# A Mamba layer and an fp8 feed-forward layer on one core: waits of the first stage reordered, twelve states of C loaded two batches earlier

## The chip, the core and the metric
The kernel runs on one core of a Trainium2 chip. Its time is the device time of one execution in microseconds (us). TensorE (PE) multiplies, VectorE (DVE), ScalarE (ACT) and GpSimd (POOL) work element by element, SyncE (SP) issues the DMA transfers. The engines run side by side and wait for each other through semaphores.

## What is computed
x has the shape (4, 512, 512): batches, positions, features. The result is x plus a Mamba layer of the normalized x plus a gated feed-forward layer of the normalized x. Cut to what matters:

```python
xn = layernorm(x)
# Mamba: DI 1024, N 16 states, R 128
proj = einsum('blh,eh->bel', xn, Win); hs, gate = proj[:, :DI], proj[:, DI:]
hs = silu(conv4(hs) + bconv)                      # causal, 4 taps, per channel
ssm = einsum('bdl,pd->blp', hs, Wx)               # dt_in (128), B (16), C (16)
dt = softplus(einsum('blr,dr->bld', dt_in, Wdt) + bdt)
h_t = exp(A * dt_t) * h_(t-1) + dt_t * B_t * hs_t # for each channel and state
y = (sum_n h * C + hs * D) * silu(gate)
out = x + einsum('bdl,hd->blh', y, Wout)
# feed-forward in fp8, HIDDEN 2048
out += qdot(gelu(qdot(xn, w_g0)) * qdot(xn, w_g1), w_lin)
```

## The kernel before, in words
The program has two stages. The first (`stage_a`) makes, for each of the 4 batches `b`, the transposed normalized x (`xnT`), the projection `hs` of 8 units `k` of 128 channels, the convolution, silu, the small projections (`dt_ps` for dt, `bc_ps` for B and C), and `dt` and `dt*hs` (`dt_du`). It stores them in DRAM. The second (`stage_b`) walks over batches, units and 16 states: a scan on VectorE for each state (line 1125), with exp on ScalarE (`da`) and `dt*hs*B` on GpSimd (`dbu`).

Products in the first stage are made of a high and a low part of each operand (`products`): ScalarE makes the high parts (`hs_hi`, `xnT_hi`), the low parts (`hs_lo`, `xnT_lo`) are differences, made by GpSimd but for the start. In a batch TensorE makes units 2 to 7 of the projection, three units ahead of the products `ssm_inputs(k)` of hs; then dtin is copied (ScalarE, line 597), and the softplus stretch follows: for each unit TensorE makes z (`project_dt`), VectorE `capped`, ScalarE Exp and Ln, VectorE `dt_du` (line 495), GpSimd its product with hs (`du`, line 378), SP the store. `dt_du` has four slots; `dt_du(k)` waits for the store of `dt_du(k-4)`. Beside it TensorE begins the next batch's projection: tile h of unit 0 after z of unit h+2, then units 1 and 2.

Every transfer is issued by SP, in the order in which its program is written, on one queue. In a batch before the change: the store of xnT (1 MB), for units 0, 3 and 6 a `chunk` (store of the converted fp8 weights `w8`, 256 KB, and load of the next `wf`, 1 MB, which VectorE converts behind its convolutions of units 1, 4 and 7, line 473), for each unit the store of hs (256 KB), xn8, bc, the eight stores of dt_du (512 KB each), the load of four states of B (`b_head`, 1 MB). In the last batch six loads of C of batch 0 (`c_head`, two states and 512 KB each) and two of `unit` (768 KB) are interleaved. `c_head` holds the rows of x of batches 1 to 3 (`x_rest`) until they are normalized, four states of it for each batch.

At the end of the first stage GpSimd makes the first six `dbu` of the second (`head_start`, three instructions, line 858) ahead of its last eight du. `deviation` is the square root of the variance `vare` of the next batch; its function lies in another table of ScalarE than silu.

## Time and profile before

| | |
|---|---|
| median of 3 runs | 1058.67 us (1058.31 to 1058.89) |
| profiled execution | 1060.56 us, its span 1058.8 us |
| VectorE busy | 994.5 us (94%) |
| GpSimd busy | 913.0 us (86%) |
| TensorE busy | 910.5 us (86%) |
| ScalarE busy | 832.8 us (79%) |
| granted TensorE clock, mean | 0.956 |
| first scan of the second stage | 206.07 us |

The span runs from the first to the last instruction of the profiled execution. A busy share is a mean over both stages; the granted clock is the share of full speed that TensorE had.

### The profile page before, as it was taken

The page shows a single profiled execution, that of the slowest core. Times are in us where ns is not written, and L with a number is a line of the kernel's source. Part 1 is how long each engine was busy: PE and PEld are TensorE (multiplying, and loading weights), DVE is VectorE, ACT ScalarE, POOL GpSimd, SP SyncE. Part 2 cuts the span into 40 slices and gives each one's busy share as a digit, 9 for nine tenths or more (in the row PEclk, how much of TensorE's full clock was granted, in tenths as well). Part 3 has the DMA queues.
Part 4 walks back from the last instruction along what each step waited for, and adds up shares of the span by engine and source line. Part 5 has one row for each costly group of instructions (what it writes and reads, how often), then busy time and mean ns, then how long its engine had stood idle before and what let it go on. Part 6 is the DMA issues. An engine that isn't in the chain of part 4 may idle for free.

```text
span 1058.8 us, 14443 instructions
## 1 busy us (share of the span) xinstructions
PE 910.5 (86%) x4328; PEld 561.2 (53%) x4328; DVE 994.5 (94%) x1190; ACT 832.8 (79%) x1164; POOL 913.0 (86%) x512
## 2 busy tenths in 40 slices
PE   5888989577789987998799879887998798879998
PEld 4656757244445554554455556554555455445554
DVE  6887878799999999999999999999999999999996
ACT  5888987688888666898896668988866689888662
POOL 4566674899999899899999998999899989998993
PEclk9999999889889998999999979998999899999999
DMA  8678879991112129232121292221213922212101
GB/s 305 219 264 281 302 264 345 377 334 55 61 41 90 40 75 332 107 103 80 60 90 41 97 346 88 86 80 60 90 41 115 350 78 75 80 59 81 41 1 40
DMA packets 53208, 150.26 MB, mean 142 GB/s; under 512 B 5776, under 2 KB 14096, under 8 KB 50064
## 3 DMA queue, kind: packets, MB, share of 16 engines
q1 hardware_dynamic: 53136, 149.41, 40.6%
q8 instruction: 32, 0.52, 0.2%
q14 instruction: 40, 0.33, 0.1%
HBM read 111.37 MB, written 38.01 MB: 141 GB/s over the span
## 4 chain that ended last, share of the span: by engine, by line
DVE 32%; issue 25%; POOL 17%; ACT 11%; PE 7%; DMA 6%; SPq 1%; DVEq 1%; POOLq 0%; ACTq 0%
POOL dbu L858 11%; DVE da L1125 11%; DVE prod L1100 8%; DVE hp L1125 6%; POOL hp L1088 4%; DMA wf<-in_wffn 3%; ACT da L1019 2%; DVE conv L445 2%; PE yT L1251 2%; ACT L1008 1%; ACT L1007 1%; DVE gate_bf L1138 1%; DVE y L1108 1%; PE mm L1200 1%; DMA b_all<-bc_d 1%
## 5 line engine op out<-in xcount | busy, mean ns | idle before, releaser
L1019 ACT ACTIVATE da<-unit,neg_a 128x512 f32<-128x512 f32 x512 | 338.6, 684 | 156.9 <-DVE prod L1100 154.0
L858 POOL TENSOR_TENSOR dbu<-unit,b_head 128x1024 f32<-128x1024 f32 x192 | 450.0, 2367 | 0.0
L1125 DVE TENSOR_TENSOR_SCAN da<-da,dbu 128x512 f32<-128x512 f32 x352 | 417.9, 1218 | 1.3
L1251 PE MATMUL yT<-ident,prod 128*128 128x128 f32 x1408 | 227.7, 291 | 93.0 <-DVE prod L1100 92.2
L1251 PEld LDWEIGHTS yT<-ident,prod 128*128 128x128 f32 x1408 | 168.2, 147 | 227.7 <-DVE prod L1100 188.2
L1088 POOL TENSOR_TENSOR hp<-hp,c_head 128x512 f32<-128x512 f32 x128 | 162.7, 1271 | 50.7 <-DVE gate_bf L1141 46.1
L1125 DVE TENSOR_TENSOR_SCAN hp<-da,dbu 128x512 f32<-128x512 f32 x160 | 193.5, 1210 | 3.3 <-ACT da L1019 3.3
L1100 DVE TENSOR_TENSOR prod<-da,c_head 128x512 f32<-128x512 f32 x256 | 171.7, 671 | 0.0
L1200 PE MATMUL mm<-xn_b,w_sb 128*128 128x512 fp8e4 x512 | 143.8, 414 | 15.9 <-ACT acc L1039 12.9
L858 POOL TENSOR_TENSOR dbu<-unit,b_all 128x1024 f32<-128x1024 f32 x64 | 151.0, 2359 | 0.0
L1212 PE MATMUL mm<-xnT_b,wgate 128*128 128x512 f32 x256 | 128.8, 601 | 0.0
L1160 PE MATMUL mm<-y,wout_sb 128*128 128x512 f32 x242 | 114.6, 593 | 0.8 <-DVE y L1108 0.8
L1251 PE MATMUL yT<-ident,hp 128*128 128x128 f32 x640 | 98.9, 278 | 0.0
L1200 PEld LDWEIGHTS mm<-xn_b,w_sb 128*128 128x128 fp8e4 x512 | 51.5, 105 | 66.0 <-issue 34.7
L362 POOL TENSOR_TENSOR hs_lo<-hs,hs_hi 128x512 fp32r<-128x512 f32 x32 | 41.8, 1307 | 44.8 <-ACT hs_hi L568 44.8
L445 DVE SCALAR_TENSOR_TENSOR conv<-proj,cols_sb,conv 128x511 f32<-128x511 f32 (+2 forms) x96 | 71.0, 746 | 8.7 <-ACT conv L550 6.3
L1251 PEld LDWEIGHTS yT<-ident,hp 128*128 128x128 f32 x640 | 77.6, 145 | 0.0
L1160 PEld LDWEIGHTS mm<-y,wout_sb 128*128 128x128 f32 x242 | 43.4, 190 | 43.0 <-issue 41.9
L1100 DVE TENSOR_TENSOR prod<-da,c_all 128x512 f32<-128x512 f32 x96 | 65.0, 678 | 0.0
L1221 PE MATMUL mm<-act,w_sb 128*128 128x512 fp8e4 x256 | 61.8, 379 | 0.0
L625 PE MATMUL proj<-xnT_lo,win_hi 128*128 128x512 f32 x128 | 57.0, 446 | 0.2 <-DVE conv L445 0.2
L378 POOL TENSOR_TENSOR dt_du<-dt_du,hs 128x512 f32<-128x512 f32 x32 | 40.9, 1283 | 13.0 <-DVE dt_du L495 12.4
(123 smaller groups left out, 1285.8 us busy)
## 6 DMA issues: line engine op xcount, KB each, us to landing
unit<-unit_d SPq DMA_DIRECT2D x32, 768.0 KB, 4.2
unit_d<-dt_du SPq DMA_DIRECT2D x32, 512.0 KB, 2.9
wf<-in_wffn SPq DMA_DIRECT2D x12, 1024.0 KB, 7.1
c_head<-bc_d SPq DMA_DIRECT2D x24, 512.0 KB, 4.1
b_head<-bc_d SPq DMA_DIRECT2D x18, 512.0 KB, 4.9
unit_d<-hs SPq DMA_DIRECT2D x32, 256.0 KB, 6.6
w_sb<-w_d SPq DMA_DIRECT2D x64, 128.0 KB, 3.8
wgate<-in_win_gate SPq DMA_DIRECT2D x32, 256.0 KB, 2.7
```

The costliest lines, as they stand in the source:

```text
L445: ins = nc.vector.scalar_tensor_tensor(out=conv[:, k % 2, back:L], in0=proj[k % 3][:, 0:L - back], scalar=cols_sb[:, k, C_TAP + TAPS - 1 - ...
L625: nc.tensor.matmul(bank, hi, low, start=start, stop=False)
L858: return nc.gpsimd.tensor_tensor(dbu[:, n % DBUS:n % DBUS + NS, :], twice, b_all[n // NS], ALU.mult)
L1019: nc.scalar.activation(da[n % SLOTS][:, :], unit[:, k % 2, 0, :], ACT.Exp, scale=neg_a[:, k, n:n + 1]).then_inc(da_ready, 1)
L1088: nc.gpsimd.tensor_tensor(tile, tile, c_all[m // NS][:, m % NS, :], ALU.mult).then_inc(hp_ready, 1)
L1100: nc.vector.tensor_tensor(prod[:, slot, :], da[n % SLOTS][:, :], c_all[n // NS][:, n % NS, :], ALU.mult).then_inc(prod_ready, 1)
L1125: nc.vector.tensor_tensor_scan(state, da[n % SLOTS][:, :], dbu[:, n % DBUS, :], 0.0, ALU.mult, ALU.add).then_inc(scanned, 1)
L1160: return nc.tensor.matmul(bank[:, :], wout_sb[:, c, h * P:(h + 1) * P], y2[:, c, :], start=(c == first), stop=(c == last))
L1200: ins = nc.tensor.matmul(bank[:, :], wffn[:, k % 2, j, f, s, :].bitcast(FP8), xn8[:, f, :].bitcast(FP8), start=(f == 0), stop=(f == HT - 1))
L1212: ins = nc.tensor.matmul(bank[:, :], wgate[:, k % 2, c * P:(c + 1) * P], xnT[:, c, :], start=(c == 0), stop=(c == 3))
L1221: ins = nc.tensor.matmul(bank[:, :], wlin[:, i, h * P:(h + 1) * P].bitcast(FP8), act8[:, i, :].bitcast(FP8), start=(i == 0), stop=(i == HI ...
L1251: ins = nc.tensor.matmul(yT[k % 2][:, t * P:(t + 1) * P], product[:, t * P:(t + 1) * P], ident[:, :], start=False, stop=last, is_transpose ...
```

## The change
Four edits concern waits. SP's chunk of unit 0 comes before the store of xnT (in the last batch the xnT store comes at unit 3, and the second `unit` load at unit 4). ScalarE makes the deviation at the start of a batch, behind the tap of unit 1, with one table load less. The copies of the last xnT tile move behind two units of the softplus stretch, on ScalarE, and its low part behind two du, on GpSimd. In batches 2 and 3 the low part of hs of unit 7 is made by VectorE. Besides, the six loads of C leave the last batch: four are issued in batch 1 and two in batch 2, behind the store of hs of unit 6. SP's loop over batches is written out.

```diff
--- before.py
+++ after.py
@@ -295,25 +295,27 @@
                         wait(dt_du_stored[i], 16 * (B - 1) * (KU // DTS) + 16)
                     wait(win_split, KU)
                     wait(xn_used, B)
-                wait(xnT_ready, b * HT + HT + 2)
-                sp.dma_start(row(xnT_d, b), xnT[:, :, :].rearrange("p k l -> p (k l)")).then_inc(xnT_stored, 16)
                 for k in range(KU):
                     if k % 3 == 0:
                         chunk(k // 3)
+                    if k == (3 if last else 0):
+                        wait(xnT_ready, b * HT + HT + 2)
+                        sp.dma_start(row(xnT_d, b), xnT[:, :, :].rearrange("p k l -> p (k l)")).then_inc(xnT_stored, 16)
                     if k == KU - 1:
                         wait(xn8_ready, b + 1)
                         sp.dma_start(row(xn8_d, b), xn8[:, :, :].rearrange("p k l -> p (k l)")).then_inc(xn8_stored, 16)
                     wait(hs_ready, b * KU + k + 1)
                     sp.dma_start(row(unit_d, b * KU + k)[:, 2 * L:3 * L], hs[:, k, :]).then_inc(hs_stored[k % 2], 16)
-                    if last and k >= 2:
-
-                        g = k - 2
-                        sp.dma_start(c_head[:, g * NS:(g + 1) * NS, :].rearrange("p n l -> p (n l)"),
-                                     bc_d[0:1, N + g * NS:N + (g + 1) * NS, :].rearrange("o n l -> o (n l)").broadcast_to([P, NS * L])
-                                     ).then_inc(c_loaded[g], 16)
-                    elif last:
-
-                        u = k
+                    if k == 6 and 1 <= b < B - 1:
+
+                        wait(xn_ready, 2 * b + 4)
+                        for g in range(2 * G_PER_B) if b == 1 else range(2 * G_PER_B, G_AHEAD):
+                            sp.dma_start(c_head[:, g * NS:(g + 1) * NS, :].rearrange("p n l -> p (n l)"),
+                                         bc_d[0:1, N + g * NS:N + (g + 1) * NS, :].rearrange("o n l -> o (n l)").broadcast_to([P, NS * L])
+                                         ).then_inc(c_loaded[g], 16)
+                    if last and k in (0, 4):
+
+                        u = k // 4
                         sp.dma_start(unit[:, u, :, :].rearrange("p w l -> p (w l)"), row(unit_d, u)).then_inc(unit_loaded[u], 16)
                 wait(bc_copied, b + 1)
                 sp.dma_start(row(bc_d, b), bc[:, :]).then_inc(bc_stored, 16)
@@ -328,7 +330,8 @@
                                  bc_d[0:1, bass.ds(first, states), :].rearrange("o n l -> o (n l)").broadcast_to([P, states * L])
                                  ).then_inc(b_head_loaded, 16)
 
-            run_batches(sp, body)
+            for b in range(B):
+                body(b, b == B - 1)
             for stored in (xnT_stored, xn8_stored):
                 wait(stored, 16 * B + 16)
             wait(w8_stored, 16 * CHUNKS + 16)
@@ -357,6 +360,8 @@
 
             def body(b, last):
                 for k in range(KU):
+                    if k == KU - 1 and b >= B - 2:
+                        continue
                     pool.wait_ge(hs_hi_ready, b * KU + k + 1)
                     pool.wait_ge(ssm_summed, b * KU + k + 1)
                     nc.gpsimd.tensor_tensor(hs_lo[:, k % 2, :], hs[:, k, :], hs_hi[:, k % 2, :], ALU.subtract).then_inc(hs_lo_ready, 1)
@@ -367,15 +372,20 @@
                             ins = nc.gpsimd.tensor_scalar(xn[:, t, :], x_rest[:, b * LT + t, :], moments[:, t, 0:1], rstd[:, t:t + 1],
                                                           ALU.subtract, ALU.mult)
                         ins.then_inc(xn_ready, 1)
+                def low_tile(h):
+                    pool.wait_ge(xnT_ready, (b + 1) * HT + h + 1 + 2)
+                    nc.gpsimd.tensor_tensor(xnT_lo[:, h, :], xnT[:, h, :], xnT_hi[:, h, :], ALU.subtract).then_inc(lo_ready, 1)
+
                 if not last:
-                    for h in range(HT):
-                        pool.wait_ge(xnT_ready, (b + 1) * HT + h + 1 + 2)
-                        nc.gpsimd.tensor_tensor(xnT_lo[:, h, :], xnT[:, h, :], xnT_hi[:, h, :], ALU.subtract).then_inc(lo_ready, 1)
+                    for h in range(HT - 1):
+                        low_tile(h)
                 if last:
                     head_start(pool)
                 for k in range(KU):
                     pool.wait_ge(dt_ready, b * KU + k + 1 + KU)
                     nc.gpsimd.tensor_tensor(dt_du[:, k % DTS, 1, :], dt_du[:, k % DTS, 0, :], hs[:, k, :], ALU.mult).then_inc(du_ready, 1)
+                    if k == 1 and not last:
+                        low_tile(HT - 1)
 
             for b in range(B):
                 body(b, b == B - 1)
@@ -462,6 +472,11 @@
                 for k in range(KU):
                     if k > 0:
                         convolve(b, k)
+                    if k == KU - 1 and b >= B - 2:
+                        dve.wait_ge(hs_hi_ready, b * KU + k + 1)
+                        dve.wait_ge(ssm_summed, b * KU + k + 1)
+                        dve.wait_ge(hs_lo_ready, b * KU + k)
+                        nc.vector.tensor_tensor(hs_lo[:, k % 2, :], hs[:, k, :], hs_hi[:, k % 2, :], ALU.subtract).then_inc(hs_lo_ready, 1)
                     if k == 3 and not last:
                         scales(b + 1)
                     if k in (1, 4, 7):
@@ -567,9 +582,13 @@
                     act.wait_ge(ssm_summed, b * KU + k + 1)
                     nc.scalar.activation(hs_hi[:, k % 2, :], hs[:, k, :], ACT.Copy).then_inc(hs_hi_ready, 1)
 
+                newest_tap(b, 1)
+                if not last:
+                    deviation(b + 1)
                 nc.scalar.preload_act_table_set("silu_and_others")
                 for k in range(1, KU):
-                    newest_tap(b, k)
+                    if k > 1:
+                        newest_tap(b, k)
                     if k == 5 and not last:
                         act.wait_ge(scales_ready, b + 2)
                         act.wait_ge(xn_used, b + 1)
@@ -579,9 +598,6 @@
                         ins.then_inc(xn_ready, 1)
                     silu(k - 1)
                     high_part(k - 1)
-                    if k == 2 and not last:
-                        deviation(b + 1)
-                        nc.scalar.preload_act_table_set("silu_and_others")
                     if k == 4:
                         fp8_copy(b)
 
@@ -597,9 +613,9 @@
                 nc.scalar.activation(dtin[:, :], dt_ps[:, :], ACT.Copy).then_inc(dtin_copied, 1)
                 nc.scalar.activation(bc_low[:, :], bc_ps[2 * N:4 * N, :], ACT.Copy).then_inc(bc_low_copied, 1)
                 nc.scalar.preload_act_table_set("natural_log_exp_and_others")
-                if not last:
-                    copy_tiles(b + 1, HT - 1, HT)
                 for k in range(KU):
+                    if k == 2 and not last:
+                        copy_tiles(b + 1, HT - 1, HT)
                     act.wait_ge(z_ready, b * KU + k + 1)
                     nc.scalar.activation(soft[:, k % 3, :], soft[:, k % 3, :], ACT.Exp).then_inc(exp_done, 1)
                     act.wait_ge(exp_done, b * KU + k + 1)
```

ScalarE, start of batch 0, before: the table load, the tap of unit 1 (`conv<-proj`), silu and high part of units 0 and 1, then the deviation between its two table loads.
```order
L570 ACT_TABLE_LOAD
L550 ACTIVATE conv<-proj,cols_sb 128x512
L563 ACTIVATE hs<-conv 128x512
L568 ACTIVATE hs_hi<-hs 128x512
L550 ACTIVATE conv<-proj,cols_sb 128x512
L563 ACTIVATE hs<-conv 128x512
L568 ACTIVATE hs_hi<-hs 128x512
L525 ACT_TABLE_LOAD
L525 ACTIVATE sd<-vare 128x4
L584 ACT_TABLE_LOAD
```
After:
```order
L565 ACTIVATE conv<-proj,cols_sb 128x512
L540 ACT_TABLE_LOAD
L540 ACTIVATE sd<-vare 128x4
L588 ACT_TABLE_LOAD
L578 ACTIVATE hs<-conv 128x512
L583 ACTIVATE hs_hi<-hs 128x512
L565 ACTIVATE conv<-proj,cols_sb 128x512
L578 ACTIVATE hs<-conv 128x512
L583 ACTIVATE hs_hi<-hs 128x512
L565 ACTIVATE conv<-proj,cols_sb 128x512
```
The deviation with both loads stands ahead of the first silu (`hs<-conv`), and one load is gone.

SP, end of batch 1: the transfers from the load of the last chunk on, before (the loop's body, the same for batches 0 to 2):
```order
L262 DMA wf<-in_wffn 128x2048
L254 REGISTER_ALU
L307 ISA
L307 DMA unit_d<-hs 128x512
L254 REGISTER_ALU
L305 DMA xn_d<-xn 128x2048
L254 REGISTER_ALU
L307 ISA
L307 DMA unit_d<-hs 128x512
L319 ISA
L319 DMA bc_d<-bc 32x512
```
After, batch 1:
```order
L262 DMA wf<-in_wffn 128x2048
L308 DMA unit_d<-hs 128x512
L313 DMA c_head<-bc_d 128x1024 x4
L306 DMA xn_d<-xn 128x2048
L308 DMA unit_d<-hs 128x512
L321 DMA bc_d<-bc 32x512
L324 DMA unit_d<-dt_du 128x1024 x8
L329 DMA b_head<-bc_d 128x2048
```
Four loads of C stand ahead of the stores of xn8, of hs of unit 7, of bc and of all dt_du.

VectorE, end of the last batch: the last convolution (three instructions), the conversion of the last weights, the sum of B and C, before:
```order
L445 SCALAR_TENSOR_TENSOR conv<-proj,cols_sb,conv 128x511
L445 SCALAR_TENSOR_TENSOR conv<-proj,cols_sb,conv 128x510
L445 SCALAR_TENSOR_TENSOR conv<-proj,cols_sb,conv 128x509
L473 TENSOR_SCALAR w<-wf 128x2048
L489 TENSOR_TENSOR bc<-bc_ps,bc_low 32x512
```
After:
```order
L455 SCALAR_TENSOR_TENSOR conv<-proj,cols_sb,conv 128x511
L455 SCALAR_TENSOR_TENSOR conv<-proj,cols_sb,conv 128x510
L455 SCALAR_TENSOR_TENSOR conv<-proj,cols_sb,conv 128x509
L479 TENSOR_TENSOR hs_lo<-hs,hs_hi 128x512
L488 TENSOR_SCALAR w<-wf 128x2048
L504 TENSOR_TENSOR bc<-bc_ps,bc_low 32x512
```
hs_lo stands between the convolution and the conversion.

## Rows read from the trace of the kernel before

**Rows 1.** Windows: us, busy PE, PEld, DVE, ACT, POOL, PEclk, DMA share, GB/s
```profile
206.00:1059.00 853.00, 739.44 (x3656) 442.34 (x3656) 835.90 (x941) 670.47 (x922) 784.98 (x415) 0.95 0.31 105
```

**Rows 2.** Timeline of VectorE: start us, us, line, operation [idle before, releaser]
```profile
19.34 1.91 DVE L438 TENSOR_TENSOR wx_lo<-wf,wx_hi 128x1024 fp32r<-128x1024 f32 x1 [1.60 <-ACT wbc L544]
...
27.23 0.17 DVE L405 TENSOR_SCALAR vare<-moments 128x4 f32<-128x4 f32 x1
...
55.04 0.97 DVE L405 TENSOR_SCALAR vare<-moments 128x4 f32<-128x4 f32 x1
...
178.06 1.23 DVE L473 TENSOR_SCALAR w<-wf 128x2048 fp8e4<-128x2048 f32 x1 [4.35 <-DMA wf<-in_wffn]
...
201.27 0.75 DVE L495 SCALAR_TENSOR_TENSOR dt_du<-dt_ps,cols_sb,soft 128x512 f32<-128x512 f32 x1 [1.68 <-DMA unit_d<-dt_du]
...
206.07 1.22 DVE L1125 TENSOR_TENSOR_SCAN da<-da,dbu 128x512 f32<-128x512 f32 x1
```

**Rows 3.** Timeline of TensorE: products of hs that begin a batch, transposes
```profile
30.27 0.47 PE L625 MATMUL dt_ps<-hs_lo,wx_hi 128*128 128x512 f32 x1 [2.80 <-POOL hs_lo L362]
...
76.62 0.47 PE L625 MATMUL dt_ps<-hs_lo,wx_hi 128*128 128x512 f32 x1 [0.47 <-POOL hs_lo L362]
...
93.40 1.03 PE L620 MATMUL tp<-ident,unit 128*128 128x128 f32 x8
...
121.64 0.40 PE L625 MATMUL dt_ps<-hs_lo,wx_hi 128*128 128x512 f32 x1
...
166.35 0.39 PE L625 MATMUL dt_ps<-hs_lo,wx_hi 128*128 128x512 f32 x1
```

**Rows 4.** Timeline of ScalarE: table load, silu, dtin copies, last tile, Ln, deviation
```profile
25.41 1.28 ACT L570 ACT_TABLE_LOAD   x1
...
27.39 0.62 ACT L563 ACTIVATE hs<-conv 128x512 f32<-128x512 f32 x1
...
55.03 0.60 ACT L597 ACTIVATE dtin<-dt_ps 128x512 f32<-128x512 f32 x1 [0.93 <-PE bc_ps L666]
...
101.14 0.60 ACT L597 ACTIVATE dtin<-dt_ps 128x512 f32<-128x512 f32 x1 [1.11 <-PE bc_ps L666]
...
103.67 0.60 ACT L514 ACTIVATE xnT_hi<-tp 128x512 fp32r<-128x512 f32 x1
...
115.52 0.63 ACT L606 ACTIVATE soft<-soft 128x512 f32<-128x512 f32 x1
...
123.50 0.21 ACT L525 ACTIVATE sd<-vare 128x4 f32<-128x4 f32 x1
...
145.81 0.60 ACT L597 ACTIVATE dtin<-dt_ps 128x512 f32<-128x512 f32 x1 [0.89 <-PE bc_ps L666]
...
190.15 0.60 ACT L597 ACTIVATE dtin<-dt_ps 128x512 f32<-128x512 f32 x1 [2.25 <-PE bc_ps L666]
```

**Rows 5.** DMA of the window 168 to 192 us
```profile
DMA packets 2457, 9.36 MB, mean 390 GB/s; under 512 B 270, under 2 KB 270, under 8 KB 1974
```

**Rows 6.** Timeline of SP: last w8 store of batch 1
```profile
98.77 0.33 SPq L287 DMA_DIRECT2D w_d<-w  x1
```

**Rows 7.** DMA of the window 103 to 104 us; issue, KB, us to landing
```profile
DMA packets 31, 0.25 MB, mean 254 GB/s; under 512 B 0, under 2 KB 0, under 8 KB 0
...
bc_d<-bc SPq DMA_DIRECT2D x1, 64.0 KB, 4.6
```

**Rows 8.** DMA issued between 99.0 and 99.6 us
```profile
wf<-in_wffn SPq DMA_DIRECT2D x1, 1024.0 KB, 6.5
```

**Rows 9.** Timeline of GpSimd: low part of the weights, of xnT, head start
```profile
17.61 2.56 POOL L356 TENSOR_TENSOR win_lo<-win_rest,win_hi 128x512 fp32r<-128x512 f32 x2 [3.15 <-ACT win_hi L532]
...
53.46 3.75 POOL L373 TENSOR_TENSOR xnT_lo<-xnT,xnT_hi 128x512 fp32r<-128x512 f32 x3
...
188.61 7.96 POOL L858 TENSOR_TENSOR dbu<-unit,b_head 128x1024 f32<-128x1024 f32 x3
```

**Rows 10.** Windows of TensorE, 32 to 34 us: busy (products), clock, DMA share, GB/s
```profile
32.00:34.00 2.00, 2.00 (x6) 0.50 0.94 242
```

## The prediction
> **What bounds the kernel now.** I read the windows first, to split the span. From 206 us on, VectorE is busy 835.90 of 853 us, against 739 on TensorE, 785 on GpSimd and 670 on ScalarE [rows 1]: the second stage runs at VectorE's own pace. It begins with the first scan at 206.07 [rows 2]. No edit touches its orders, so the change is worth what it moves that first scan by. The profiled execution took 1060.56 us beside its span of 1058.8; it stands 1.9 us above the median of the runs, 1058.67. I make the sum within the span and put the difference on the median. A measurement here tells 0.2%, some 2.1 us, from no change.
>
> Within the first stage I read the timeline of each engine. Every batch has two parts. From the first product of a unit's hs on TensorE (S) to the end of the last projection TensorE never waits: from 76.62 to the transposes at 93.40, where 1.14 of that is the fifth group of products (their pitch in the rows around), so S plus 15.65 us [rows 3]. Behind that the last unit goes through tap, convolution, silu, high part, low part and products to the copy of dtin (D). Behind D comes the softplus stretch, in which ScalarE, VectorE, TensorE and the stores of dt_du form one ring of four slots, until the next S. The rows give S = 30.27, 76.62, 121.64, 166.35 and D = 55.03, 101.14, 145.81, 190.15 [rows 3, 4]. So D to S takes 21.6, 20.5, 20.5, and S to D 24.8, 24.5, 24.2, 23.8. The last D to the first scan is 15.9.
>
> **Part by part, in order of time.**
>
> *Batch 0, the deviation first.* Before, the table load at 25.41 ends at 26.7 and the first silu starts at 27.39 [rows 4]. Now the tap comes at 25.41 (0.67), a load of 1.28, then sd. It waits for vare, written at 27.23 + 0.17 [rows 2]; sd 0.2 [rows 4], a second load 1.28: first silu at 28.95, +1.55. TensorE was waiting for just this unit (2.80 idle before 30.27) and runs full behind it, so S0 and D0 move by +1.55.
>
> *Softplus stretch.* Before, the last tile's copies stand at 103.67, two of 0.6 with a pitch of 0.97, ahead of the first Exp [rows 4]. Moved behind two units they let dt_du(0) come 0.9 sooner. TensorE, then VectorE and ScalarE pass on some 0.7: the last Ln ends at D + 14.3 instead of D + 15.0 (115.52 + 0.63 against 101.14). GpSimd's fourth low tile (1.25) fits behind du(1), since TensorE asks for it at D + 9.0. Behind the last Ln ScalarE now has tap 0.67, two loads and sd 2.8, silu 0.66, high part 0.7, then GpSimd 1.3: S at D + 20.6. In the last batch there is one load only, and TensorE is later: D + 19.9. The two loads that vanish in the middle of a batch, around the sd at 123.50 [rows 4], lay beside a full TensorE and are worth nothing; were TensorE not full there, they would be worth up to 2.6. Batch 0 had 21.6, so it gains 1.0; S1 comes at +0.55.
>
> *Weight chunk.* VectorE waited 4.35 for a chunk at 178.06 [rows 2], and less in the two batches before. The xnT store (1 MB) leaves its way. At 390 GB/s, the rate of the full queue from 168 to 192 [rows 5], that is 2.6 us sooner; in batch 1 the chunk now lands before VectorE asks. The last batch then follows TensorE again. The tail from the last projection to D is 7.3 (batch 0 has 7.4, with nothing in its way) against 8.9 in batch 1: -1.55. So D1 = -1.0.
>
> *C in batches 1 and 2: the disputed cost.* The rows of batch 1: the w8 store issues at 98.77, the bc store issues just behind 103 and lands 4.6 us later, at 107.9 [rows 6, 7]. Four loads of C (512 KB, 1.3 us each at the same rate) are put ahead of xn8, hs(7) and bc: 5.2 us. (SP's new wait for xn passes at once: xn of the next batch is made two units earlier.) The queue is then empty at D + 11.35; the first dt_du store goes behind it and lands 1.3 later, D + 12.65. Its slot is wanted by dt_du(4) at D + 10.0. That ring turns 2.6 late: dt_du(4) ends at D + 13.3, the last Ln at D + 16.6, z of unit 7, which waits for dt_du(4), starts at D + 13.3 on TensorE, and S at D + 23.2. Against 20.5 that is +2.65. S2 = +1.65.
> In batch 2 only two C loads come, 2.6 us. But the hs_lo that VectorE takes over stands ahead of its last w8, so the w8 store moves from D - 2.85, where batch 1 will have it, to D - 0.15, and the queue is again full until D + 11.3. dt_du(4) waits for D + 12.6, TensorE's z likewise, and three projections (8.2) end at D + 22.4: +1.85. In return hs_lo itself takes 0.7 instead of 1.3 to 1.5 there, and the wait for the chunk is gone: the tail is 6.75 against 8.6, -1.85. D2 = -0.2, S3 = +1.65.
>
> *Last batch.* The tail: GpSimd, freed of the last hs_lo, starts its head start (three dbu, 7.96 in all, the first of them held up) at once instead of at 188.61 [rows 9]. It begins 3.35 behind the last projection; VectorE wants its hs_lo at 4.5. Does GpSimd hold it up? wx_lo, 1024 elements on VectorE with both inputs in SBUF, started at 19.34 and took 1.91, with GpSimd's win_lo in SBUF until 17.61 + 2.56 = 20.17: what is left is 1.08. And vare took 0.97 at 55.04 beside a row of GpSimd's xnT_lo, 0.17 at 27.23 [rows 2, 9]. So I take it that hs_lo waits for the end of the first dbu (2.34), runs 0.7 and ends 6.4 behind the projection. D3 is then 7.85 behind it against 8.15: -0.3. If it didn't wait, 6.6: -1.55.
> The Trainium skill has a rule for it (SBUF — State Buffer, Who interferes with whom): a VectorE instruction with two SBUF inputs and a GpSimd one that reads SBUF fully block each other, and the first to issue wins. By that rule the sum is the one with the wait; the rows agree.
> From D3 on: before, dt_du(4) waited 1.68 for the first store, at 201.27; that store's du stood behind the head start, which ends at 196.57 [rows 2, 9], with C loads in the queue ahead of it. Now the head start ends by D + 4.5, no C is in the queue, the store lands by D + 9.3, and dt_du(4) is wanted at D + 9.4. The first scan comes at D + 14.25 against 15.92: -1.67.
>
> **Sum**: +1.55 - 1.0 - 1.55 + 2.65 - 1.85 + 1.85 + (S3 to D3) -0.3 - 1.67 = -0.3 us (rounded). SP's unrolled loop saves a few tenths of issue time per batch, hidden behind the same full queue; its cover gone it is worth 0.3. Forecast 1058.67 - 0.35 = **1058.3 us**: what the four changes give, about 4, C's new place takes back.
>
> **The rivals.**
> *C hides (faster).* The chunk ahead of C's new place took 6.5 us from issue for 1 MB [rows 8], where the full queue's rate makes 2.6: the queue has holes there, and C may fill them. In the window from 103 on it moved 254 GB/s, not 390 [rows 5, 7]. All bytes at 390 GB/s from the w8 store on: 4.06 MB, 10.4 us, the queue is empty at D + 9.2 and dt_du(4) waits 0.5 instead of 2.6; in batch 2, 0.65. Then D1 to S2 is 20.9 and D2 to S3 20.5, the sum -4.4: 1054.3. Against it: in the batches before each small store behind a chunk landed with it, in order, so C would begin only behind it. The Trainium skill says that descriptors of a ring start in order but are pipelined (DMA: Bandwidth & Descriptors, Queues, rings and completion order). By that this rival is possible; no row settles it.
> *TensorE's clock falls (slower).* After 2.80 us idle at 27.5 the granted clock fell from 30.9 to 34.3; at 32 it is 0.50, 1.2 GHz instead of 2.4, six products in 2 us instead of nine [rows 3, 10]. That costs half of 3.4 us, 1.7. With dt_du(4) 2.6 late TensorE idles 2.65 between z(6) and z(7), in batches 1 and 2. If it falls in both, +3.4: 1061.7; in one, 1060.0. [...]
> *hs_lo isn't held up*: -1.25, 1057.0, within "no change". The deviation's +1.55 in batch 0 could be less only if vare came sooner, which nothing does.
>
> **Chances.** Forecast with its own range 1056.6 to 1059.8: 0.50. C hides, in part or all: 0.30. Clock falls at least once: 0.18. The rest 0.02. Most of the forecast's range lies within 0.2%, 0.06 of it is faster; partial cases of the clock in one batch fall on the edge. So faster 0.36, same 0.46, slower 0.18, and the range from 1054.4 to 1060.8 leaves out about one in ten on each side.
>
> **What would show it.** The changed profile: first silu near 28.9; no wait of VectorE for a chunk in batch 1; dt_du in batches 1 and 2 waiting some 2 us for its store (if not, C hides); hs_lo on VectorE in the last batch about 1.9 long (0.7 would refute the blocking); the granted clock between D and S of batches 1 and 2; no wait for a store behind the last D; the first scan at 205.7. Wrong would make it above all a queue that doesn't keep order, or a second stage that isn't the same length (852.7 from the first scan on).

## The result: 0.7% slower

The changed kernel took 1066.01 us (median of 4, 1065.75 to 1069.42) against 1058.78 us for the kernel before on the same chip: ratio 1.0073, interval 1.0055 to 1.0090. A second measurement (run after_again, below) gave 1.0075, 1.0062 to 1.0088. The forecast was 1058.3 us, with a range up to 1060.8: the loss is real, 7 to 8 us, and lies outside it.

The profiled execution of the changed kernel is a long one of its kind, 1069.42 us with a span of 1067.3. Single executions of one kernel differ here: the kernel before took 1057.5 to 1061.7 us in 25 runs. So the profiles say where the time goes, and the medians say how much of it is real.

First the page after, its row of the clock over 40 equal slices of the span (a digit is the granted clock in tenths, 9 stands for 0.9 or more), then the window of the second stage (as in [rows 1]) and VectorE's timeline around the last batch's end (start us, us, line, operation, idle before and its releaser; as in [rows 2]):

```profile
PEclk9899998978899998999989988999999899989999
```

```profile
214.70:1067.00 852.30, 741.97 (x3646) 443.79 (x3656) 835.80 (x941) 670.55 (x922) 785.11 (x415) 0.95 0.31 105
```

```profile
114.55 0.75 DVE L510 SCALAR_TENSOR_TENSOR dt_du<-dt_ps,cols_sb,soft 128x512 f32<-128x512 f32 x1 [2.34 <-DMA unit_d<-dt_du]
...
162.81 0.75 DVE L510 SCALAR_TENSOR_TENSOR dt_du<-dt_ps,cols_sb,soft 128x512 f32<-128x512 f32 x1 [2.82 <-DMA unit_d<-dt_du]
...
196.24 1.69 DVE L479 TENSOR_TENSOR hs_lo<-hs,hs_hi 128x512 fp32r<-128x512 f32 x1 [1.36 <-ACT hs_hi L583]
197.86 3.39 DVE L488 TENSOR_SCALAR w<-wf 128x2048 fp8e4<-128x2048 f32 x1
201.17 0.67 DVE L504 TENSOR_TENSOR bc<-bc_ps,bc_low 32x512 f32<-32x512 f32 x1
...
214.78 1.22 DVE L1141 TENSOR_TENSOR_SCAN da<-da,dbu 128x512 f32<-128x512 f32 x1
```

The first scan stands at 214.78 instead of 206.07 [rows 2], and VectorE is as busy behind it as before, 835.80 us against 835.90 [rows 1]. So all of it is lost in the first stage. As in the prediction, D is the start of a batch's copy of dtin and S the first product of the next unit's hs, each with the number of its batch. dt_du(4) waits for its store in batches 1 and 2, 2.34 and 2.82 us, and starts at D + 12.5 and D + 13.0: this step stands as forecast (D + 12.65, D + 12.6). The next view shows what I had only as a rival. These are TensorE's windows (us, busy time, products, granted clock, DMA share, GB/s):

```profile
28.00:30.00 2.00, 0.00 (x0) 0.95 0.00 0
30.00:32.00 2.00, 0.00 (x0) 0.50 0.07 27
32.00:34.00 2.00, 1.66 (x4) 0.50 1.09 231
...
114.00:116.00 2.00, 0.65 (x1) 0.78 1.04 424
116.00:118.00 2.00, 2.00 (x4) 0.50 0.88 354
118.00:120.00 2.00, 2.00 (x9) 0.87 0.97 393
...
162.00:164.00 2.00, 0.39 (x1) 0.73 1.02 418
164.00:166.00 2.00, 2.00 (x4) 0.50 0.91 369
...
168.00:170.00 2.00, 2.00 (x7) 0.57 0.52 209
```

Behind each of the two waits the clock stands at 0.50, 1.2 GHz, with six products or fewer in 2 us; before, it stood there only in batch 0 [rows 10] and from 205 us on. TensorE's own rows at those places, and the first product of batch 0:

```profile
32.34 0.76 PE L641 MATMUL dt_ps<-hs_lo,wx_hi 128*128 128x512 f32 x1 [5.55 <-POOL hs_lo L367]
...
115.35 2.08 PE L689 MATMUL dt_ps<-dtin,wdt_sb 128*128 128x512 f32 x2 [2.39 <-DVE dt_du L510]
...
163.61 2.08 PE L689 MATMUL dt_ps<-dtin,wdt_sb 128*128 128x512 f32 x2 [2.87 <-DVE dt_du L510]
```

In batch 0 TensorE idles 5.55 us where it idled 2.80 [rows 3]. ScalarE's timeline of that place, and the four copies of dtin (D; before in [rows 4]):

```profile
23.78 0.63 ACT L547 ACTIVATE win_hi<-win_rest 128x512 fp32r<-128x512 f32 x1 [0.84 <-DMA win_rest<-in_win_hs]
...
25.10 1.28 ACT L540 ACT_TABLE_LOAD   x1
27.64 0.20 ACT L540 ACTIVATE sd<-vare 128x4 f32<-128x4 f32 x1 [1.25 <-DVE vare L415]
27.86 1.28 ACT L588 ACT_TABLE_LOAD   x1
29.15 0.63 ACT L578 ACTIVATE hs<-conv 128x512 f32<-128x512 f32 x1
...
57.51 0.60 ACT L613 ACTIVATE dtin<-dt_ps 128x512 f32<-128x512 f32 x1 [0.94 <-PE bc_ps L682]
...
102.08 0.60 ACT L613 ACTIVATE dtin<-dt_ps 128x512 f32<-128x512 f32 x1 [0.92 <-PE bc_ps L682]
...
149.84 0.60 ACT L613 ACTIVATE dtin<-dt_ps 128x512 f32<-128x512 f32 x1 [0.29 <-PE bc_ps L682]
...
199.46 0.60 ACT L613 ACTIVATE dtin<-dt_ps 128x512 f32<-128x512 f32 x1 [2.65 <-PE bc_ps L682]
```

The first silu, at 29.15, is within 0.2 us of the forecast. But the load of weights ahead of it landed a microsecond sooner in this execution (win_hi at 23.78, before at 24.76), so silu stands 5.37 behind that cast (`win_hi`) where it stood 2.63: measured from there, the edit costs ScalarE 2.7, not 1.55.

With S = 32.34, 78.92, 127.31 and 175.88 the profiled stage goes so, term by term (us, measured difference of the two profiles):

| stretch | forecast | measured |
|---|---|---|
| to S0 | +1.55 | +2.07 |
| S0 to D0 | 0 | +0.41 |
| D0 to S1 | -1.0 | -0.18 |
| S1 to D1 | -1.55 | -1.36 |
| D1 to S2 | +2.65 | +4.73 |
| S2 to D2 | -1.85 | -1.64 |
| D2 to S3 | +1.85 | +5.50 |
| S3 to D3 | -0.3 | -0.22 |
| D3 to the first scan | -1.67 | -0.60 |
| sum | -0.3 | +8.71 |

The three tails (S to D) are right within 0.2 in this execution. The stretches that begin at D carry the miss: 7.6 of the 9.0 us beyond the forecast.

The first tail did not come out so each time. In the profiled execution of after_again, the same kernel once more, D0 to S1 took 22.47 us and S1 to D1 24.74, 1.1 and 1.6 more than here. VectorE's conversion of a weight chunk, GpSimd's first hs_lo of batch 1, TensorE's product behind it, and TensorE's window:

```profile
77.60 1.22 DVE L488 TENSOR_SCALAR w<-wf 128x2048 fp8e4<-128x2048 f32 x1
77.62 2.32 POOL L367 TENSOR_TENSOR hs_lo<-hs,hs_hi 128x512 fp32r<-128x512 f32 x1 [0.79 <-ACT hs_hi L583]
80.19 0.47 PE L641 MATMUL dt_ps<-hs_lo,wx_hi 128*128 128x512 f32 x1 [2.15 <-POOL hs_lo L367]
82.00:84.00 2.00, 2.00 (x6) 0.50 1.01 397
```

The conversion started 0.02 us ahead of hs_lo, which took 2.32 instead of 1.27 (in the first profile hs_lo was first, and the conversion took 2.25). TensorE idled 2.15 us instead of 1.10, and its clock fell behind that. So the two profiles of one kernel differ by some 2.6 us here through the order of two starts and the clock.

### The profile page after: what moved, and what is told of

Read it like the earlier page. It is cut to its first block, busy times and chain, and to the rows that moved or that the text cites. A ratio compares the mean times of both kernels' runs of the same rounds, so it can differ in the third digit from the quotient of the medians.

```text
span 1067.3 us, 14211 instructions
## 1 busy us (share of the span) xinstructions
PE 919.6 (86%) x4318; PEld 565.6 (53%) x4328; DVE 1000.8 (94%) x1192; ACT 828.9 (78%) x1161; POOL 913.7 (86%) x510
## 4 chain that ended last, share of the span: by engine, by line
DVE 44%; issue 23%; PE 16%; ACT 10%; DMA 3%; POOL 3%; DVEq 1%; SPq 0%; POOLq 0%
DVE da L1141 18%; DVE prod L1116 12%; DVE hp L1141 9%; PE yT L1267 3%; ACT da L1035 2%; PE mm L1176 2%; DMA unit_d<-dt_du 2%; DVE y L1124 2%; POOL dt_du L386 1%; ACT L1024 1%; ACT L1023 1%; PE proj L642 1%; PE proj L641 1%; PE proj L643 1%; PE mm L1228 1%
```

## The experiments

There are four groups; the kernels of one group shared a chip and the kernel before. All ratios are against the kernel before.

**Group 1: which half of the change?** c_only is the kernel before with C's new place alone:

```diff
-                    if last and k >= 2:
-                        g = k - 2
+                    if k == 6 and 1 <= b < B - 1:
+                        wait(xn_ready, 2 * b + 4)
+                        for g in range(2 * G_PER_B) if b == 1 else range(2 * G_PER_B, G_AHEAD):
...
-            run_batches(sp, body)
+            for b in range(B):
+                body(b, b == B - 1)
```

> The kernel before with C's new place alone (and SP's loop written out, which it needs). Theory A (C's place makes the loss, through the queue and then through TensorE's clock): the store of dt_du(0) lands some 2.6 us late in batch 1 and less in batch 2, TensorE idles 2.4 to 2.9 us in front of z(7), and its granted clock falls behind that; D to S takes 24.5 to 26 us in both batches instead of 20.5, some 1.1 comes back behind the last D: 6 to 9 us slower than before, 1065 to 1068. Theory B (the queue alone, as I forecast: 2.65 and 1.85, and the rest of the loss sits in the four edits of waits): 3 us slower, 1062.

Measured: 1062.63 against 1059.51, ratio 1.0025 (1.0016 to 1.0034). Theory B by its size, though not term by term (below). waits_only is the other half, the changed kernel with C loaded at k >= 2 of the last batch:

> The changed kernel with C's loads back in the last batch: the four edits of waits alone. Theory A: batch 0 loses 2.5 (deviation first, and TensorE's slow clock), the tails of batches 1 and 2 give back 1.4 and 1.65, the softplus stretches 0.2 each, the last tail nothing: 1 to 2 us faster than before, 1057 to 1058. Theory B: the four edits lose 3 to 5 us: 1062 to 1064.

Measured: 1063.95, ratio 1.0038 (1.0025 to 1.0050). The four edits that I had down as a gain of about 4 us lose 4.4 by themselves. Both halves lose. That 3.1 and 4.4 add up to the loss of the whole (7.2) is partly chance: waits_only has a long wait for a store in the last batch that the whole lacks (below), and the whole has a wait for a store in batch 2 and a low clock behind z(7) that neither half has. In c_only's profile dt_du(4) waits for its store only in batch 1:

```profile
113.12 0.75 DVE L497 SCALAR_TENSOR_TENSOR dt_du<-dt_ps,cols_sb,soft 128x512 f32<-128x512 f32 x1 [2.05 <-DMA unit_d<-dt_du]
```

There D1 to S2 is 22.69, 2.2 more than before; D2 to S3 is 20.51, as before. TensorE idles 2.09 us in front of z(7) and the clock stays at 1.00 behind it. The other microsecond is in S3 to D3 (24.85 against 23.80). waits_only also shows what C costs in its old place once xnT's store stands at unit 3 of the last batch, in VectorE's timeline (before, the same row waited 1.68, [rows 2]):

```profile
204.90 0.75 DVE L509 SCALAR_TENSOR_TENSOR dt_du<-dt_ps,cols_sb,soft 128x512 f32<-128x512 f32 x1 [2.43 <-DMA unit_d<-dt_du]
```

c_early keeps the whole change, but issues C one unit sooner, ahead of the last weight chunk:

```diff
-                    if k == 6 and 1 <= b < B - 1:
+                    if k == 5 and 1 <= b < B - 1:
```

> The changed kernel with C's loads one unit earlier: behind hs(5) instead of hs(6), so ahead of the last weight chunk. The queue is empty there from 94 to 99 and from 143 to 149 us. Theory A: C hides in that gap, no dt_du waits over 1 us for a store in batches 1 and 2, the clock stays full, D to S is 20.5 again: 1 to 3 us faster than before, 1056 to 1058. Theory B: only 4.5 us come back, 1061 to 1062. If C's bytes lengthen the weight chunk behind them all the same, about 1066.

Measured: 1061.10, ratio 1.0012 (1.0003 to 1.0021), by the ratios some 6 us less than the changed kernel and 2.8 less than waits_only. Between the two theories: C hides in the gap in this profile; the loss of the four edits stays, less what C cost waits_only in the last batch. In the view of VectorE's waits (line, releaser, us in total, times, longest) this is all that is left for dt_du's stores:

```profile
DVE dt_du L510 <- DMA unit_d<-dt_du: 0.2, 1, 0.2
```

warm fills TensorE's idle time in front of z(7) with products that nothing reads:

```diff
+                    if k == KU - 1 and not last:
+                        for _ in range(8):
+                            nc.tensor.matmul(tp[0][:, :], win_hi[:, 0, 0:P], xnT_hi[:, 0, :], start=True, stop=True)
                     if k >= 3:
                         pe.wait_ge(dt_ready, b * KU + k - 2 + KU)
```

> The changed kernel, and in front of z(7) of batches 0 to 2 TensorE runs eight products of 512 columns (about 0.24 us each, 1.9 in all) into a bank that nothing reads: the idle time of 2.4 and 2.9 us shrinks to 0.5 to 1. The store is as late as before. Theory A: the granted clock stays full behind z(7), and of the loss the clock's part comes back, some 4 to 5 us: 1061 to 1062. Theory B: the clock has no share in it, the products change nothing: 1066, or slower where they stand in front of a z that is ready.

Measured: 1067.55, ratio 1.0074 (1.0061 to 1.0087). By the median, theory B. Its profile says otherwise of two places: D1 to S2 is 24.31 and D2 to S3 22.89, against 25.23 and 26.04, with the clock at 1.00 in both; but D0 to S1 is 22.91 instead of 21.41, since in batch 0 z(7) was hardly late and the products held it up: it started at D + 12.6 instead of D + 11.0. The products were badly placed, and warm12 below does it again.

**Group 2: which of the four edits?** dev_only is the kernel before with sd's activation at the start of the batch; dev_back is the changed kernel without that edit:

```diff
+                newest_tap(b, 1)
+                if not last:
+                    deviation(b + 1)
                 nc.scalar.preload_act_table_set("silu_and_others")
...
-                    if k == 2 and not last:
-                        deviation(b + 1)
-                        nc.scalar.preload_act_table_set("silu_and_others")
```

> The kernel before with one edit alone: sd's activation behind tap(1), ahead of the first silu. Theory A (this edit is the larger part of what the four edits of waits lose): the first silu of batch 0 waits for vare and for a second table load, TensorE idles over 5 us there and its clock falls for longer, +2 to +3.5; the stretches from D0 to S1 and from D1 to S2 have two table loads ahead of silu instead of one, up to +1.5 each, of which the waits for weight chunks later in the batch may swallow some: 3 to 6 us slower than before. Theory B (it costs 1.55 once, as I forecast; the loss is in the order of the stores and copies): 1.5 us slower.

> The changed kernel with that one edit taken back: sd's activation behind unit 1 again. Theory A: 3 to 6 us faster than the changed kernel, so 1.5 to 4.5 us slower than the kernel before, which is left to C's place. Theory B: 1.5 us faster than the changed kernel, 6 slower than before.

Measured: dev_only 1064.03 against 1059.60, ratio 1.0038 (1.0025 to 1.0051); dev_back 1062.10, ratio 1.0031 (1.0017 to 1.0046). Theory A both times: the edit costs 4.4 us by the medians (4.0 by the ratio) put in, and some 4.5 by the ratios taken out. ScalarE's timeline shows how, in dev_only ahead of S2 and in the kernel before at the same place:

```profile
117.96 0.63 ACT L607 ACTIVATE soft<-soft 128x512 f32<-128x512 f32 x1
118.87 0.78 ACT L550 ACTIVATE conv<-proj,cols_sb 128x512 f32<-128x512 f32 x1 [0.28 <-PE proj L628]
119.67 1.28 ACT L525 ACT_TABLE_LOAD   x1
120.97 0.21 ACT L525 ACTIVATE sd<-vare 128x4 f32<-128x4 f32 x1
121.19 1.28 ACT L573 ACT_TABLE_LOAD   x1
122.48 0.63 ACT L563 ACTIVATE hs<-conv 128x512 f32<-128x512 f32 x1
```

```profile
116.17 1.28 ACT L570 ACT_TABLE_LOAD   x1
117.46 0.78 ACT L550 ACTIVATE conv<-proj,cols_sb 128x512 f32<-128x512 f32 x1
118.14 0.62 ACT L563 ACTIVATE hs<-conv 128x512 f32<-128x512 f32 x1
```

From the end of the last Ln to the first silu it is 3.89 us instead of 1.99 (118.14 less the end of Ln, 115.52 + 0.63, [rows 4]). TensorE waits for just this silu. The loads saved in the middle of the batch lay beside a full TensorE.

early_dev_back undoes both losses, C at k == 5 and sd behind unit 1; early_dev_pool also gives the last batch's last hs_lo back to GpSimd (`b >= B - 2` becomes `b == B - 2` on both engines).

> The changed kernel with sd's activation behind unit 1 again and C's loads behind hs(5). Theory A: both losses are gone and the other three edits bring their 2 to 4 us: 1 to 4 us faster than before, 1055.5 to 1058.5 where before has 1059.5. Theory B: no faster than before.

> As early_dev_back, and hs_lo of the last batch's last unit is made by GpSimd again (batch 2's stays on VectorE). In the changed kernel it took 1.69 us and the weight chunk behind it 3.39 us, both beside GpSimd's first products of dbu. Theory A: the blocked stretch costs about 1 us on the path to D and the first Exp, but GpSimd's head start then begins a unit later, and its du with it: within 1 us of early_dev_back, either way. If the blocking is dear: 1 to 2 us faster. If the late head start is dear: 1 to 2 us slower.

Measured: early_dev_back 1056.66, ratio 0.9971 (0.9959 to 0.9982), faster than before by 2.9 us; early_dev_pool 1056.55, ratio 0.9977 (0.9963 to 0.9991). Against dev_back, C one unit sooner is worth 5.4 us by the medians, 6.4 by the ratios. It is not free there: in the profile of early_dev_back VectorE waits 1.59 us for batch 1's last chunk, dt_du(4) still waits 0.85 for its store, and D1 to S2 takes 22.80. What remains of the change, the other three edits and C in the earlier batches, is a gain. Where the last hs_lo is made makes no difference that these runs can tell (1056.66 and 1056.55, single executions from 1053.5 to 1062.6); that the blocking and the earlier head start cancel is my reading, not shown.

**Group 3: the clock's share, and a better kernel.** after_again is the changed kernel once more. warm12 has the eight products in batches 1 and 2 only.

> The changed kernel once more, beside the next one on the same chip: 7 to 8 us slower than the kernel before.

> The changed kernel with the eight products in front of z(7) of batches 1 and 2 alone (TensorE's batches written out for it, no longer a loop); in batch 0, where they had held z(7) up and stretched D0 to S1 by 1.5 us, there are none. Theory A (TensorE's clock, falling behind the wait for the late store, has a share in what C's place costs): D to S takes 24.3 and 22.9 us in batches 1 and 2 as in the first such run, 2 to 4 us faster than the changed kernel. Theory B (the queue alone): no faster than it.

Measured: after_again 1068.42 against 1059.56, ratio 1.0075; warm12 1066.45, ratio 1.0058 (1.0046 to 1.0070): 2 us faster than the changed kernel beside it. That is theory A, at the low end of its size, but the two intervals touch and TensorE's batches are written out besides; the share of the clock is shown by the stretches below rather than by the median. VectorE's row of dt_du(4) in batches 1 and 2 of warm12, then TensorE's windows behind those waits, and third the same windows of after_again:

```profile
115.44 0.75 DVE L510 SCALAR_TENSOR_TENSOR dt_du<-dt_ps,cols_sb,soft 128x512 f32<-128x512 f32 x1 [3.04 <-DMA unit_d<-dt_du]
...
161.96 0.75 DVE L510 SCALAR_TENSOR_TENSOR dt_du<-dt_ps,cols_sb,soft 128x512 f32<-128x512 f32 x1 [2.80 <-DMA unit_d<-dt_du]
```

```profile
116.00:118.00 2.00, 1.76 (x6) 1.00 0.99 406
118.00:120.00 2.00, 2.00 (x11) 1.00 0.85 340
...
164.00:166.00 2.00, 2.00 (x10) 1.00 0.88 356
```

```profile
118.00:120.00 2.00, 1.74 (x4) 0.72 0.98 399
120.00:122.00 2.00, 2.00 (x6) 0.50 0.83 334
...
168.00:170.00 2.00, 2.00 (x6) 0.50 0.96 387
```

The wait for the store is no shorter, yet the clock stays at 1.00, and D to S takes 24.19 and 22.92 us instead of 25.37 and 24.58. This splits what C's place costs, profile against profile: without the late store the same stretches took 21.71 and 20.15 (c_early), so the queue costs 2.5 and 2.8 us, and the clock another 1.2 and 1.7 (in the first profile of the changed kernel 1.0 and 3.1). Over all profiles without the products, TensorE idled 2.31 to 2.93 us in front of z(7) of batches 1 and 2 seven times, and the clock fell each time; after 1.88 to 2.11 us it stayed at 1.00, three times of three (in the last batch it fell even after 1.88 to 2.00). With the products it stayed at 1.00, four times of four.

even33 is early_dev_back with three loads of C in each batch; even33_fill0 fills TensorE's idle time in batch 0 as well:

```diff
-                        for g in range(2 * G_PER_B) if b == 1 else range(2 * G_PER_B, G_AHEAD):
+                        for g in range(3 * b - 3, 3 * b):
...
+                    if k == 3 and b == 0:
+                        for _ in range(8):
+                            nc.tensor.matmul(tp[0][:, :], win_hi[:, 0, 0:P], xnT_hi[:, 0, :], start=True, stop=True)
                     if k >= 3:
                         ssm_inputs(k - 3)
```

> As early_dev_back, with three of C's loads in each of batches 1 and 2 instead of four and two. In early_dev_back the weight chunk and bc's copy of batch 1 still came about a microsecond late and dt_du(6) or (4) waited 0.9 for a store; 1.3 us less in that queue should take most of it: 0 to 1.5 us faster than early_dev_back, 3 to 4.5 us faster than before. If batch 2 then has the late store instead: no change, 3 faster than before.

> As even33, and TensorE runs eight products that nobody reads in batch 0, where it waits 2.8 to 3.4 us for hs_lo(0) (TensorE's batches written out for it). Theory A: its clock then doesn't fall at 31 us, D0 to S0 is 23.2 instead of up to 25.9: 1 to 1.5 us faster than even33 by the median. Theory B (the clock has no share): no change.

Measured: even33 1057.72, ratio 0.9976 (0.9966 to 0.9986), no better than early_dev_back: in its profile dt_du(4) waits 2.06 us for a store in batch 2 instead, as the second guess said. even33_fill0 1054.27, ratio 0.9955 (0.9942 to 0.9968): 5.3 us faster than before, and faster than even33 by 3.4 us (by the ratios 2.2), more than I expected of it. Its TensorE timeline and windows at the place, to be held against [rows 3] and [rows 10]:

```profile
27.41 1.98 PE L695 MATMUL tp<-xnT_hi,win_hi 128*128 128x512 f32 x8
29.40 0.50 PE L640 MATMUL dt_ps<-hs_lo,wx_hi 128*128 128x512 f32 x1
```

```profile
30.00:32.00 2.00, 2.00 (x10) 1.00 0.10 39
32.00:34.00 2.00, 2.00 (x10) 1.00 1.05 219
```

Its first scan stands at 199.68, 6.4 us ahead of before. S0 to D0 takes 23.51 where before it took 24.76. But even33 had 23.56 there in its profiled execution, and early_dev_back 23.17 after TensorE had idled 3.35 us, both at a clock of 1.00 without the products: the clock doesn't fall there every time. So one profile can't show that the products kept it up in batch 0. Of the 3.41 us between the first scans of the two profiles, 2.02 lie in D2 to S3, where even33's wait for the store is gone, and 1.06 in S3 to D3; none lies ahead of D0. Why even33_fill0 is faster stays open: the products, TensorE's batches being written out, which I didn't try alone, or both.

**Group 4: who pays?** dev_batch0 and dev_later are the kernel before with sd's activation first in batch 0 alone, and in batches 1 and 2 alone. hs_lo_b2_back is the changed kernel with batch 2's last hs_lo on GpSimd (`b >= B - 2` becomes `b == B - 1`).

> The kernel before, with sd's activation behind tap(1) in batch 0 alone. Theory A (most of what that edit costs is in batch 0: the first silu waits for vare and a second table load, then TensorE's clock): 2.3 us slower than before, as S0 stood 2.25 later with the edit in all batches. Theory B (it is the second table load in the stretches from D to S of the later batches): 1.5 us or less.

> The kernel before, with sd's activation behind tap(1) in batches 1 and 2 alone. Theory A: 1.5 us slower than before, in the stretch from D1 to S2, of which the wait for the weight chunk in batch 2 swallows a part. Theory B: 3 us slower.

> The changed kernel, with hs_lo of batch 2's last unit on GpSimd again (the last batch's stays on VectorE). Theory A (that hs_lo, ahead of VectorE's last chunk, puts the w8 store 2.7 us later, and C's two loads with it, so that batch 2's first dt_du store is late only through it): no wait of dt_du(4) in batch 2 as in c_only, D2 to S3 5 us shorter, the tail 0.7 to 1 longer: 2 to 4.5 us faster than the changed kernel, 1062 to 1065. Theory B (C's loads make the store late in any case): within 1 us of the changed kernel.

Measured against 1060.03: dev_batch0 1062.74, ratio 1.0026 (1.0017 to 1.0034); dev_later 1060.63, ratio 1.0007 (0.9998 to 1.0016). So batch 0 pays 2.7 us of it, and the later batches 0.6, within no change; together somewhat less than dev_only's 4.4. In dev_later's profile, one of its longest executions (1062.52), D0 to S1 is 1.24 longer (hs_lo is held up by VectorE's chunk as in after_again, and TensorE idles 2.15 us), D1 to S2 is 1.75 longer, and the tail behind that 1.0 shorter, where VectorE's wait for its last chunk is gone (0.47 in dev_batch0).

hs_lo_b2_back 1065.66, ratio 1.0050 (1.0035 to 1.0064): by the ratios 2.6 us faster than the changed kernel, at the edge of the intervals. Theory A, by its profile above all: D2 to S3 takes 20.27 us instead of 24.58 and 26.04. Its VectorE row of batch 2, and SyncE's issue of the weight chunk's store:

```profile
163.51 0.75 DVE L510 SCALAR_TENSOR_TENSOR dt_du<-dt_ps,cols_sb,soft 128x512 f32<-128x512 f32 x1 [0.15 <-DMA unit_d<-dt_du]
```

```profile
150.37 0.32 SPq L287 DMA_DIRECT2D w_d<-w  x1
```

With D2 = 153.21 the store is issued at D - 2.84, in the changed kernel at D - 0.28, and the wait of 2.82 is gone. C's two loads alone make no late store in batch 2 (c_only had none there either); they collide because VectorE's hs_lo stands ahead of the chunk.

## Why the prediction was wrong, point by point

- *Batch 0, the deviation first*, "+1.55 ... so S0 and D0 move by +1.55". This term is mis-sized: dev_batch0 measures +2.7, with D0 2.02 later in its profile. The silu waits for vare, and I took vare's time as fixed at 27.40. VectorE makes it behind the unit's convolution, so it moves with everything ahead of it; in the run c_early it came at 28.88. And TensorE, idle 5.55 us instead of 2.80, ran at the low clock until 37: S0 to D0 grew by 0.41 in the changed kernel's profile, by 0.85 in dev_batch0's.
- *Softplus stretch*, S "at D + 20.6". With C out of the way (c_early) it was D + 21.4 and D + 21.7. The last Ln did come sooner, but I set the tap right behind it, and it waits 0.4 us for TensorE's projection; from silu to S it took 2.9 and 3.2 us, not 2.7. dev_later and dev_only show the later batches' part of that: two table loads stand where TensorE waits. What I did not see at all is that the later silu brings GpSimd's hs_lo beside VectorE's chunk (after_again, above).
- *Weight chunk and tails*, -1.55, -1.85, -0.3: right in mechanism, and in size in the first profile, -1.36, -1.64, -0.22. No chunk was waited for in batch 1 in either profile; in the second the low clock behind S1 made the first of them +0.22.
- *C in batches 1 and 2*, "+2.65" and "+1.85". The queue's part is right in mechanism and in size: I had S at D + 20.6 and D + 19.9 without C and at D + 23.2 and D + 22.4 with it, so 2.6 and 2.5, and measured are 2.5 and 2.8. The reason I gave for batch 2, hs_lo ahead of the chunk, is shown by hs_lo_b2_back. What failed is the step that put the clock at nothing in the sum. I had it as a rival with 0.18, beside a row in which it fell after 2.80 us idle, and summed a forecast with 2.65 us of just such idle time in it. It fell after 2.39 and 2.87 us, and in the second profile after 2.43 and 2.69, at 1.0 to 3.1 us each. The forecast and that rival were not alternatives: the one makes the other. So D1 to S2 came out 2.1 above the forecast by 1.1 of the deviation's stretch (above) and 1.0 of the clock, and D2 to S3 3.65 above it, 3.1 of them by the clock. The rival *C hides* is refuted for this place. One unit sooner it holds in c_early's profile, and only in part in early_dev_back's.
- *hs_lo in the last batch* "about 1.9 long": 1.69, against 0.69 in batch 2. It is blocked, as forecast. What I left out is the chunk behind it, 3.39 us beside a running dbu of GpSimd instead of 1.53, its time before, when it had started first (at 188.20, the head start at 188.61 [rows 9]): bc and the first Exp come late. The Trainium skill (SBUF — State Buffer, Who interferes with whom) lists tensor_scalar among the operations that can take the shared ports; these times agree.
- *D3 to the first scan*, "-1.67": measured -0.60. dt_du(4) has no wait for its store, as forecast; the late chunk and a low clock at 200 to 204 stand in the rest (early_dev_back, at a clock of 1.00 until its first scan, took 14.79 against the forecast 14.25). Against waits_only (18.38) C's absence is worth 3 us there.
- *The second stage* has the same length, 852.5 against 852.7.

So two steps failed: the deviation's price, 1.55 once where it measures about 4.4, and the clock, 0 where the wait for the store pulls it down in both batches. By the medians the deviation first costs about 4.4, C behind hs(6) instead of hs(5) about 5.4, and the rest of the change brings about 2.9; that makes +6.9 of the measured 7.2. (By the ratios 4.0, 6.4 and -3.1, 7.3 of 7.7. Only the deviation's price was measured apart; the other two are steps between kernels without it.) Open: how the 2.9 splits over xnT's store, the copies, hs_lo and C, which were not tried singly, and how often the clock falls in executions that weren't profiled.

## What to carry to other kernels

A wait that is forecast for the engine whose clock can fall is not paid once: price the slow stretch behind it in the same sum, not as a rival. Before an operation is moved to the start of a stage to save a table load, ask which of the two places the bound engine waits for; a load beside a full engine is free, the same load ahead of what it waits for is not. And put extra transfers where the queue is empty, looked up in the windows, and ahead of the large one: against their old place in the last batch (waits_only) C's loads lost some 4 us behind hs(6), and gained some 3 one unit sooner. Even there look at the chunk behind them, which came 1.59 us too late in early_dev_back.

## What the runs showed that I had not expected

Behind eight products of 512 columns with no reader, 2.4 us in waits of 2.8 to 3.0, the granted clock stayed at 1.00 each time in batches 1 and 2; without them it fell all seven times that TensorE idled 2.31 to 2.93 us there. And a conversion of 2048 columns on VectorE took 3.39 us instead of 1.53 while GpSimd ran its dbu: longer than one of these (8.45 us for three).
